# Split products and a transposed adapter product in the second phase of an attention and feed-forward kernel

## The reference

```
s = silu(c @ w_gate.T)                      # c: the attention's output, 1376 gate values per token
_, idx = top_k(-abs(s), 688)                # the 688 smallest in magnitude of each row
s[idx] = 0                                  # are dropped
h = s * (c @ w_up.T)
x1 = x + h @ w_down.T                       # the down product, 1376 x 512
y = x1 @ weight[adapter_id].T               # the adapter product, 512 x 512
out = x1 + y @ W4.T + b                     # W4, b: unpacked from 4 bits and scaled
```

## Time and profile before

| | |
|---|---|
| median of 3 runs | 1397.92 us (1397.61 to 1399.25) |
| profiled execution | 1399.51 us, span 1397.7 us |
| TensorE busy | 1376.4 us, 98% |
| VectorE busy | 1181.5 us, 85% |
| ACT busy | 880.4 us, 63% |
| GpSimd busy | 795.0 us, 57% |
| mean granted clock of TensorE | 0.996 of 2.4 GHz |

### The profile page before, as it was taken

How to read it: one execution, slowest core, us unless ns; L and a number is a source line. 1 busy time by engine, 2 the same in 40 slices (tenths; PEclk the granted TensorE clock), 3 DMA queues, 4 the chain that set the end, 5 groups by cost and what they waited for, 6 DMA issues and landing times.

```text
span 1397.7 us, 22868 instructions
## 1 busy us (share of the span) xinstructions
PE 1376.4 (98%) x7762; PEld 1159.6 (83%) x7762; DVE 1181.5 (85%) x2580; ACT 880.4 (63%) x2236; POOL 795.0 (57%) x832
## 2 busy tenths in 40 slices
PE   8899999999999999999999999999999999999998
PEld 6788888888888888888888888888888786667766
DVE  8989898989898989898989898999899887766662
ACT  6677676767676767676767676767777742222221
POOL 6867666666666666666676666666666500221211
PEclk9899999999999999999999999999999999999999
DMA  6111211111121112111211121212121203211121
GB/s 229 58 31 32 75 62 31 56 51 61 33 75 34 60 33 75 33 62 32 73 36 61 31 76 31 61 31 72 31 72 32 103 20 124 72 46 46 48 64 49
DMA packets 27408, 80.42 MB, mean 58 GB/s; under 512 B 9522, under 2 KB 10546, under 8 KB 23954
## 3 DMA queue, kind: packets, MB, share of 16 engines
q1 hardware_dynamic: 10898, 45.29, 9.2%
q0 software_dynamic: 16384, 33.59, 8.1%
HBM read 76.74 MB, written 2.10 MB: 56 GB/s over the span
## 4 chain that ended last, share of the span: by engine, by line
PE 89%; DVE 7%; issue 2%; ACT 2%; another core or an unknown queue 0%; POOL 0%; ACTq 0%; DVEq 0%
PE proj_ps L110 9%; PE proj_ps L112 9%; PE proj_ps L111 9%; PE turn_ps L750 9%; PE score_ps L112 5%; PE value_ps L110 5%; PE value_ps L111 5%; PE value_ps L112 5%; PE score_ps L111 5%; PE score_ps L110 5%; PE out_ps L932 5%; PE gu_ps L112 3%; PE gu_ps L110 3%; PE gu_ps L111 3%; PE turn_ps L712 2%; PE turn_ps L719 2%
## 5 line engine op out<-in xcount | busy, mean ns | idle before, releaser
L521 POOL DMA_INDIRECT kg<-kc,idx x256 | 260.7, 1018 | 277.9 <-issue 263.2
L1193 ACT ACTIVATE probs<-probs,shift,rstd 128x640 f32<-128x640 f32 x256 | 234.5, 918 | 137.3 <-DVE shift L1544 135.0
L531 POOL DMA_INDIRECT vg<-vc,idx x256 | 259.0, 1012 | 70.7 <-issue 70.7
L1580 DVE TENSOR_TENSOR pt_lo<-turn_ps,pt_hi 128x512 fp32r<-128x512 f32 x320 | 217.2, 686 | 44.6 <-ACT pt_hi L1199 39.1
L1555 DVE CUSTOM_DVE_ANT_0 probs<-score_ps,mask 128x640 f32<-128x640 f32 x256 | 208.7, 821 | 38.8 <-PE score_ps L112 35.6
L1199 ACT ACTIVATE pt_hi<-turn_ps 128x512 fp32r<-128x512 f32 x320 | 186.4, 593 | 86.6 <-PE turn_ps L750 77.4
L750 PE MATMUL turn_ps<-cst,probs 128*128 128x128 f32 x1280 | 192.7, 273 | 1.7 <-DVE qt_lo L1532 0.9
L110 PE MATMUL proj_ps<-w_hi,xt_parts 128*128 128x256 f32 (+1 forms) x500 | 190.4, 381 | 1.4 <-issue 1.4
L750 PEld LDWEIGHTS turn_ps<-cst,probs 128*128 128x128 f32 x1280 | 158.0, 141 | 28.5 <-DVE probs L1573 2.3
L112 PE MATMUL proj_ps<-w_hi,xt_parts 128*128 128x256 f32 (+1 forms) x500 | 169.6, 339 | 0.0
L111 PE MATMUL proj_ps<-w_lo,xt_parts 128*128 128x256 f32 (+1 forms) x500 | 168.6, 337 | 0.0
(11 more groups left out here) (214 smaller groups left out, 3213.5 us busy)
## 6 DMA issues: line engine op xcount, KB each, us to landing
w_raw<-wqkv SPq DMA_DIRECT2D x7, 1536.0 KB
wo_raw<-wo SPq DMA_DIRECT2D x8, 1024.0 KB
wa_sb<-wa SPq DMA_DIRECT2D x7, 1024.0 KB, 4.8
kg<-kc,idx POOLq DMA_INDIRECT x256
vg<-vc,idx POOLq DMA_INDIRECT x256
wg_raw<-wg SPq DMA_DIRECT2D x2, 1376.0 KB
wu_raw<-wu SPq DMA_DIRECT2D x1, 2752.0 KB
wd_sb<-wd SPq DMA_DIRECT2D x1, 2560.0 KB, 9.7
```

The costliest lines, as they stand in the source:

```text
L521: pool.indirect_dma_start(kg[:, b % 2, c, :], None, kc, bass.IndirectOffsetOnAxis(ap=idx[:, s // B % 2, b * NC + c:b * NC + c + 1], axis=0))\
L531: pool.indirect_dma_start(vg[:, b % 2, c, :], None, vc, bass.IndirectOffsetOnAxis(ap=idx[:, s // B % 2, b * NC + c:b * NC + c + 1], axis=0))\
L1193: act.activation(row, row, ACT.Exp, bias=shift[:, h:h + 1], scale=rstd[:, b % 2, h:h + 1], accum_out=sums[:, h:h + 1])\
L1580: dve.tensor_tensor(pt_lo[:, at, :], turn_ps[1 - j % 2][:, :], pt_hi[:, at, :].bitcast(F32), ALU.subtract).then_inc(p_lo_done[j], 1)
```

## The change

The down product becomes a split product, the adapter product is formed transposed, and the small work around both moves.

- **Down product.** Each chunk is three float32r matmuls instead of one f32 matmul. The weights get a high part (ACT) and a low part (VectorE), in parts 8 to 9, 4 to 7, 0 to 3 and the last chunk of 96 rows, as their places come free. Batch 0 has chunks 0 to 3 and 10 still plain, batch 1 chunk 10. ACT's copy of h out of PSUM becomes the rounded high part, and VectorE subtracts it from PSUM for the low part, piece by piece (`split_h`).
- **Where `split_h` stands on VectorE.** For batch i − 1, with i over 2: piece 0 after `pick_near(i)`, pieces 1 and 2 after `pick_edge(i)`. The third transposition of h waits for piece 0, and the down product waits at its first chunk for piece 1.
- **Adapter.** The weights become the stationary operand, taken with a step of two columns, and x1 the moving one: 16 matmuls of 128 columns instead of 4 of 512. y comes out transposed, so `turn_y`, ACT's two copies around it and GpSimd's `y_lo` go; ACT rounds from PSUM, and VectorE splits from PSUM, in `pick(i)` after the first guess.
- **Attention row.** ACT rounds it from PSUM without a copy first, VectorE makes the low part after the first guess (`split_c`), and GpSimd's `front` goes.
- **Memory.** `m_sb` exists once, so `magnitudes(i)` waits for the masking of batch i − 1. h is written over s. The count's by-product goes into the second half of `w_sb`, and the masked copy waits for it. The output goes from `y` instead of `acc`, and `scale_int4` waits for the output before. The down weights but the last chunk are loaded before the last attention step ends; the last chunk after it.

```diff
@@ SP
                     sp.dma_start(pb_sb, pb).then_inc(packed_in, 16)
+                    sp.dma_start(wd_raw[:, :, :],
+                                 wd[0:(NF - 1) * P, :].rearrange("(c p) n -> p c n", p=P)).then_inc(wd_in, 16)
...
                     sp.wait_ge(acc_added, ALL_ADDED)
-                    sp.dma_start(wd_sb[:, 0:NF - 1, :],
-                                 wd[0:(NF - 1) * P, :].rearrange("(c p) n -> p c n", p=P)).then_inc(wd_in, 16)
-                    sp.dma_start(wd_sb[0:last, NF - 1, :], wd[(NF - 1) * P:FI, :]).then_inc(wd_in, 16)
+                    sp.dma_start(wd_end_raw[0:last, 0, :], wd[(NF - 1) * P:FI, :]).then_inc(wd_end_in, 16)
...
-                            sp.dma_start(out[(b - 1) * S:b * S, :], acc[:, b - 1, :]).then_inc(out_done, 16)
+                            sp.dma_start(out[(b - 1) * S:b * S, :], y[:, :]).then_inc(out_done, 16)
@@ GpSimd
                     def tile(i):
                         if i > 1:
-                            y_lo(i - 2)
                             add_int4(i - 2)
                         add_x(i - 1)
                         add_bias(i - 1)
-                        if i + 2 < B:
-                            front(i + 2)
@@ TensorE, turn_h
                         else:
-                            wait(pe, h_copied[0], i + 1)
+                            h_ready(i, 0)
+                    def h_ready(i, n):
+
+                        if n == 0:
+                            wait(pe, h_copied[0], 1)
+                        wait(pe, h_lo_done, 3 * i + n)
+                        if n == 2 and not split_down(i, NF - 1):
+                            wait(pe, h_copied[2], i + 1)
+
+                    def down_products(i, to, cols):
+
+                        t = own(i)
+                        for c in range(NF):
+                            width, first, end = FCH[c][1], c == 0, c == NF - 1
+                            raw, hi, lo = (w[0:width, cols] for w in wd_places(c))
+                            if c == 0:
+                                h_ready(i, 0)
+                                h_ready(i, 1)
+                            elif c == 8:
+                                h_ready(i, 2)
...
+                            if split_down(i, c):
+                                last = product3(pe, to, (ht_his[t][0:width, c, :], ht_los[t][0:width, c, :]), (hi, lo),
+                                                first, end)
+                            else:
+                                last = pe.matmul(to, ht_raw[0:width, c, :], raw, start=first, stop=end)
+                        last.then_inc(downed, 1)
@@ TensorE, adapter
-                        for k in range(NK):
-                            last = pe.matmul(out_pss[t], x1s[t][:, k * P:(k + 1) * P], was[t][:, k, :],
-                                             start=(k == 0), stop=(k == NK - 1))
+                        for c in range(NK):
+                            for k in range(NK):
+                                last = pe.matmul(out_pss[t][:, c * P:(c + 1) * P],
+                                                 for_int4(was[t][:, k, :])[:, c // 2, c % 2, :],
+                                                 x1s[t][:, k * P:(k + 1) * P], start=(k == 0), stop=(k == NK - 1))
...
                         up(i, 0)
-                        turn_y(i - 2)
                         up(i, 1)
@@ ACT
-                        act.activation(c_sb[:, :], front_ps[i][:, :], ACT.Copy).then_inc(ct_copied, 1)
-                        wait(act, ct_copied, i + 1)
-                        act.activation(ct_hi[i % 2][:, :], c_sb[:, :], ACT.Copy).then_inc(ct_hi_done, 1)
+                        act.activation(ct_hi[i % 2][:, :], front_ps[i][:, :], ACT.Copy).then_inc(ct_hi_done, 1)
...
                     def magnitudes(i):
                         wait(act, silu_done, i + 1)
-                        act.activation(m_sb[i % 2][:, :], s_sb[i % 2][:, :], ACT.Abs, accum_out=sum_m[i % 2][:, :])\
+                        wait(act, h_done, i)
+                        act.activation(m_sb[:, :], s_sb[i % 2][:, :], ACT.Abs, accum_out=sum_m[i % 2][:, :])\
@@ VectorE
+                    def split_h(i, n):
+
+                        t = own(i)
+                        job, c, to = HT_JOBS[n], 4 * n, h_ps(i, n)
+                        dve.wait_ge(h_copied[n], i + 1)
+                        full = sum(width == P for _, width in job)
+                        last = dve.tensor_tensor(ht_los[t][:, c:c + full, :].rearrange("p c t -> p (c t)"),
+                                                 to[:, 0:full * P],
+                                                 ht_his[t][:, c:c + full, :].rearrange("p c t -> p (c t)").bitcast(F32),
+                                                 ALU.subtract)
...
                     def pick(i):
 
-                        for guess in range(len(STEP_SIZES)):
-                            pick_guess(i, guess)
+                        pick_guess(i, 0)
+                        if i > 2:
+                            split_y(i - 2)
+                        if i > 2 and i + 1 < B:
+                            split_c(i + 1)
+                        pick_guess(i, 1)
+                        pick_guess(i, 2)
+                        if i == 2:
+                            split_h(1, 0)
+                            split_wd(2)
+                            split_h(1, 1)
+                            split_h(1, 2)
+                        if i == 3:
+                            split_wd_end()
                         pick_near(i)
+                        if i > 2:
+                            split_h(i - 1, 0)
                         pick_edge(i)
+                        if i > 2:
+                            split_h(i - 1, 1)
+                            split_h(i - 1, 2)
...
                     pick_edge(0)
+                    split_wd(1)
                     drop_lower_half(0)
+                    split_wd(0)
+                    split_h(0, 1)
+                    split_h(0, 2)
                     unpack(1)
...
                     for i in range(1, B):
                         pick(i)
                         times_up(i)
+                        if i == 1:
+                            split_y(0)
+                            split_c(3)
                         drop_lower_half(i)
```

More of the change, by code:

```diff
@@ L936, in down_last @@
-                    def down_last(half):
-                        for c in range(NF):
-                            width = FCH[c][1]
-                            if c == 0:
-                                wait(pe, h_copied[0], B)
-                                wait(pe, h_copied[1], B)
-                            elif c == 8:
-                                wait(pe, h_copied[2], B)
-                            last = pe.matmul(down_last_ps[half], hts[1][0:width, c, :],
-                                             wd_sb[0:width, c, HALVES[half]], start=(c == 0), stop=(c == NF - 1))
-                        last.then_inc(downed, 1)
+                    def h_ready(i, n):
[4 more added lines that the diff above has]
+                            wait(pe, h_copied[2], i + 1)
@@ L1361, in copy_h @@
                         full = sum(width == P for _, width in job)
-                        last = act.activation(hts[t][:, c:c + full, :].rearrange("p c t -> p (c t)"),
+                        into = ht_his[t] if split_down(i, c) else ht_raw
+                        last = act.activation(into[:, c:c + full, :].rearrange("p c t -> p (c t)"),
                                               to[:, 0:full * P], ACT.Copy)
-                        for m in range(full, len(job)):
-                            width = job[m][1]
-                            last = act.activation(hts[t][0:width, c + m, :], to[0:width, m * P:(m + 1) * P], ACT.Copy)
+                        if full < len(job):
+                            width = job[full][1]
+                            into = ht_his[t] if split_down(i, c + full) else ht_raw
+                            last = act.activation(into[0:width, c + full, :], to[0:width, full * P:(full + 1) * P],
+                                                  ACT.Copy)
                         last.then_inc(h_copied[n], 1)
@@ L1837, in pick_guess @@
                         then(dve.tensor_scalar(slope[:, :], edge[:, :], -1.0 / step, None, ALU.mult))
-                        then(below(m, edge[:, :]))
+                        then(below(edge[:, :]))
                         after()
```

299 lines of the change are left out of this document (162 added, 137 removed).

## The result

| | before | after |
|---|---|---|
| median | 1398.45 us (1397.61 to 1399.25, 4 runs) | 1418.04 us (1415.14 to 1420.88, 4 runs) |
| ratio after / before | | 1.014 (95% interval 1.0118 to 1.0163) |
| profiled execution, span | 1399.51, 1397.7 us | 1417.2, 1415.4 us |
| mean granted clock | 0.996 | 0.988 |

The account below looks back on a forecast made before the run. TensorE bounds the kernel before; after the change it waits for VectorE's low parts of h. Profiled 1399.5 + 9.4 for waits and work + 11 for clock falls = 1419.9, median 1.6 lower: 1418 us, range 1405 to 1427.

Parts of the forecast that it names:

- The wait: Before the down product in middle periods, TensorE idles 3.4 us for VectorE's piece 1; period 33.9 against 32.46, + 1.5 per batch.
- G: The end of a gate product, from which the prediction counts times within a period; 1214.81 in the trace before.
- The term for GpSimd's hold on VectorE: In VectorE's guesses and near pass, 0.98 us of a held one-column operation goes, 10.24 to 9.26, as GpSimd's work is removed.
- The adapter's part: Adapter product of 16 matmuls with 32 strided loads: + 0.4 us a batch, against 0.48 saved by dropping y's transposition.
- The last batch: TensorE goes on at G + 20.6 against 15.3 before, + 5.3; the other end terms make + 1.3 together.
- The first stretch: Up to the first adapter: down product of batch 0 saves 1.0 us, its low piece comes 0.5 late, − 0.5.
- The magnitudes: Stretch with the 96-row weight split and magnitudes waiting for the masking, with one m buffer: + 2.5 us.
- The clock: Six new TensorE gaps of 3.5 to 6 us each bring a clock fall of 1.8 us: + 11, ends 0 and 18.
- The rival without falls: VectorE's wait comes but the clock does not fall: 1397.9 + 9.4 = 1407.3 us; chance 0.12.
- The sum: All stretches without clock falls: − 0.5 + 1.6 + 2.5 + 4.5 + 1.3 = + 9.4 us.
- The rival in which TensorE stays the bound: VectorE's way to the second piece of h 3.4 us shorter, 21.2 to 17.8, giving 1384 us; chance 0.06.
- the − 14 us of work: TensorE's savings in down product, halves and y's transposition, less dearer adapters, if TensorE stayed the bound.

Follow-up runs that it names:

- Moving the pieces: Changed kernel with pieces 1 and 2 of h's low part placed before the edge search for batches 3 to 7: 1401.13 us, ratio 1.0008.
- lengthening the chain: Changed kernel with one unread 1.58 us VectorE operation between the edge search and piece 1 for batches 3 to 7: 1431.39 us, ratio 1.0223.
- filler: Changed kernel with unread matmuls before TensorE's wait for piece 1, 12 in batches 2 to 5 and 22 in batch 6: 1409.42 us, ratio 1.0072.
- the run with turn 2 moved forward: Against the kernel with pieces inside the search: batch 1's piece 0 moved behind the first guess, weight split and pieces 1, 2 behind the second: 1399.10 us.
- an order that was not in the code: Changed kernel with pieces 1 and 2 inside the edge search, behind its first maximum, instead of after it: 1395.57 us, ratio 0.9977.
- 1389.5 with those reduced: Last kernel of a series built on pieces inside the search, with weight splits in flag waits, batch 6's piece 2 later, 6 unread matmuls: 1389.49 us.
- the run with neighbouring columns: Changed kernel with the adapter's weight columns for batches 0 to 6 taken as 128 neighbouring ones, not with a step of two: 1417.71 us, ratio 1.0133.

## Why the prediction was right, and where its sizes were off

The forecast was 1418 us and the median is 1418.04. The mechanism is the one that was forecast. That the numbers agree so closely is partly luck, since the terms below differ and cancel, and the runs themselves lie between 1415 and 1421.

- **The wait.** Predicted down at G + 21.2 and TensorE there at G + 17.8; measured 20.89 and 17.70. The wait is 3.19 instead of 3.4, the period 33.72 instead of 33.9. Moving the pieces removed the wait, lengthening the chain lengthened it: the cause is shown from both sides. The term for GpSimd's hold on VectorE came out as taken off: the one-column operation takes 0.16 us (1259.63) instead of 1.13. The adapter's part was taken 0.3 us too dear: it saves 0.37 a batch, not 0.08, since the int4 product's wait for GpSimd had no term.
- **The last batch.** Predicted 5.3 us later at down(6) and 4 us given back; measured 5.0 (20.31 for 15.28 from the adapter on) and 2.7, the latter with about 1.7 us of a fall of the clock in it.
- **The first stretch.** − 0.5 predicted, + 0.4 measured. Down(0) started 0.98 us late instead of 0.5, and the adapter product had a wait of 0.33 of which the profile names no releaser, so that from down(0) to the adapter 0.56 was saved (14.11 for 14.67) and not 1.0. The sign of the total isn't settled by this: in the experiments on the changed kernel, which leave all up to there as it is, adapter 0 starts between 1181.88 and 1184.11.
- **The magnitudes.** + 2.5 for the stretch to adapter 2 contained a wait for the masking that did not occur: the pick of batch 3 began at G + 3.02 (1222.00), as in every period. Less its fall the stretch is 3.2 − 1.6 = + 1.6; with filler, where the clock stayed up, it is 34.14 us, + 1.7. The wait became real only when TensorE was made earlier, in the run with turn 2 moved forward.
- **The clock.** Predicted six falls of 1.8 us, 11 in all. The profile has five in six waits, with 3.4, 3.4, 0, 6.8, 3.4 and 6.9 us at half rate. The filler priced the last five places at 8.6 us; half of the 3.4 us at the first makes 10.3 in all by the medians, and the profiled executions give about 9. The number of falls was one too high, and two were twice as long, of which the one in the last batch passed half inside its wait. The rival without falls, 1407.3, is close to what the filler gave with its one fall left, 1409.4.
- **The sum.** Without falls + 9.4 was predicted; 17.7 − 9 = + 8.7 is left.
- **The other side.** The rival in which TensorE stays the bound wanted VectorE's way to piece 1 shorter by 3.4 us and named 1384. Shortening it by an order that was not in the code gave 1395.6, since the last batch and turn 2 kept waits of their own, and 1389.5 with those reduced. No run had the − 14 us of work in full, 9.2 at most: what is left are waits of 0.8, 0.5, 1.3 and 1.1 us for low parts of h in the first two turns and the last, and the chunks of the first batches that stay plain.

What stays open: why one wait of 3.19 us left the clock up and one of 3.16 did not. The length of the wait alone doesn't decide it: in the run with neighbouring columns a wait of 3.38 us in turn 3 left the clock up, and the same wait at the same place of the changed kernel didn't.

## What to carry to other kernels

When a product is split and a second engine has to make its low parts, the place of that step in the second engine's queue is worth more than the product's saving: put it where the consumer needs it, and inside a search or other chain if need be, with work ahead of it that covers the producer's copy. Look for windows in which that engine waits for something of its own (here 2 us for a flag), since work there is free and work taken out of them is not. A short wait on TensorE cost its length here and then up to nearly as much again through the clock (3.16 us, and a period 2.7 us longer than the one before it); where it can't be removed, matmuls that nobody reads were cheaper than idling.

## What was not expected of the hardware

- Stretches at half rate measured about 3.4, 6.8 or 10.2 us, but for some at the very end: 3.4, 3.4, 0, 6.8, 3.4 and 6.9 in the changed kernel, four times 6.8 around the middle waits of the longer chain and 10.2 around its last. Waits of 3.2 to 3.4 us gave none, the short or the middle one, those of 1.6 to 2.2 us too; waits of 4.7 us and more always gave 6.8 or more (one of 4.82 us 10.2).
- Where TensorE goes from a plain f32 product to a split one, the second row of the split one stands 0.63 us behind its first instead of 0.23, at full clock:

```profile
1176.29 1.02 PE L954 MATMUL out_ps<-wd_end_raw,ht_raw 96*128 96x512 f32 x2
1176.75 0.79 PE L110 MATMUL gu_ps<-wg_hi,ct_hi 128*128 128x512 f32 x1
1177.38 0.39 PE L111 MATMUL gu_ps<-wg_lo,ct_hi 128*128 128x512 f32 x1
1177.60 0.39 PE L112 MATMUL gu_ps<-wg_hi,ct_lo 128*128 128x512 f32 x1
```

This is no cost of the change of type. The 22 records of the old down product have a pitch of 0.43 us, and 1176.29 + 2 × 0.43 + 0.23 is 1177.38: the row of the first split matmul starts while the f32 product still runs. A plain product's end is read from the second row behind it, not from the first.
